# Linear attention as one pipeline over both entries, and the experts' weights and gates made in another order

## The reference, cut to what matters

```
# layer 2, first half (t has 4096 tokens of 128 channels for each of 2 entries)
t = t + linear_attention(layernorm(t))
    q = z @ Wq + bq;  k = z @ Wk + bk;  v = z @ Wv + bv
    kv = sum over the 4096 tokens of k * v          # one number per channel and entry
    result = q * kv
# layer 2, second half: spectral filters; layer 3, first half: causal attention
# layer 3, second half
t = t + experts(layernorm(t))
    p = softmax(z @ router_w + router_b)            # 8 experts
    top 2 of 8, their p divided by their sum        # the gates
    result = sum over the 2 of gate * (z @ expert_w[e] + expert_b[e])
```

## Time and profile before

| | us |
|---|---|
| median of 3 runs | 3167.96 (3166.44 to 3173.08) |
| profiled execution, its own time | 3164.15 |
| profiled execution, span of its instructions | 3162.4 |
| mean granted TensorE clock of it, share of full speed | 0.958 |
| TensorE busy, share of the span | 91% |
| VectorE, ScalarE, GpSimd busy | 61%, 45%, 34% |

### The profile page before, as it was taken

The page is one execution under the profiler, slowest core; times in us unless marked ns, Lnnn a source line. Parts: engine busy times, 40 slices in busy tenths (PEclk is TensorE's granted clock), DMA queues, the critical chain, the costliest instruction groups (busy, mean ns, idle before and its releaser), DMA issues. The chain is left out here.

```text
span 3162.4 us, 61588 instructions
## 1 busy us (share of the span) xinstructions
PE 2886.2 (91%) x23047; PEld 2268.1 (72%) x23047; DVE 1931.8 (61%) x3810; ACT 1436.7 (45%) x3075; POOL 1081.1 (34%) x1115
## 2 busy tenths in 40 slices
PE   5889999499976789999999999999779998999699
PEld 4667777234432559999999999899568887887455
DVE  5555567558844436666666666665457766775465
ACT  2545555221134225555555555554446675666200
POOL 3444444059914035555555555554100000000000
PEclk9999999699988799999999999999879999999699
DMA  7979784000003333444344443442200000000000
GB/s 165 176 171 181 159 182 113 6 9 1 1 3 117 127 75 80 87 84 88 80 86 88 83 89 79 87 88 54 64 7 1 1 1 1 1 1 1 8 24 30
DMA packets 419407, 213.43 MB, mean 67 GB/s; under 512 B 326260, under 2 KB 398604, under 8 KB 417324
## 3 DMA queue, kind: packets, MB, share of 16 engines
q1 hardware_dynamic: 401248, 199.32, 28.8%
q10 hardware_dynamic: 17868, 10.19, 1.7%
HBM read 177.82 MB, written 52.89 MB: 73 GB/s over the span
## 5 line engine op out<-in xcount | busy, mean ns | idle before, releaser
L1754 DVE TENSOR_TENSOR sl_vl_slot<-sl_psV_slot,sl_vh_slot 128x512 fp32r<-128x512 f32 x1024 | 635.7, 683 | 381.3 <-ACT sl_vh_slot L1736 379.4
L1736 ACT ACTIVATE sl_vh_slot<-sl_psV_slot 128x512 fp32r<-128x512 f32 x1024 | 529.6, 604 | 512.0 <-PE sl_psV_slot L1691 511.2
L1709 PE MATMUL sl_psY_slot<-sl_vl_slot,sp_Mh_sp 64*128 64x512 f32 x2048 | 430.8, 389 | 0.8 <-DVE sl_vl_slot L1754 0.3
L1709 PE MATMUL sl_psY_slot<-sl_vh_slot,sp_Mh_sp 64*128 64x512 f32 x2048 | 428.2, 386 | 0.0
L1709 PE MATMUL sl_psY_slot<-sl_vh_slot,sp_Ml_sp 64*128 64x512 f32 x2048 | 428.1, 386 | 0.0
L1667 POOL TENSOR_TENSOR sl_fl_slot<-sl_f_slot,sl_fh_slot 128x512 fp32r<-128x512 f32 x256 | 337.0, 1317 | 20.5
L1665 POOL CAST sl_fh_slot<-sl_f_slot 128x512 fp32r<-128x512 f32 x256 | 167.0, 652 | 450.9 <-PE sl_psV_slot L1691 449.5
L2150 DVE TENSOR_TENSOR ca_ptl_ca<-ca_psT_ca,ca_pth_ca 128x512 fp32r<-128x512 f32 (+1 forms) x272 | 183.8, 676 | 169.1 <-ACT ca_pth_ca L2087 169.1
L2087 ACT ACTIVATE ca_pth_ca<-ca_psT_ca 128x512 fp32r<-128x512 f32 (+1 forms) x272 | 159.0, 585 | 183.4 <-PE ca_psO_ca L87 180.1
L1709 PEld LDWEIGHTS sl_psY_slot<-sl_vl_slot,sp_Mh_sp 64*128 64x128 f32 x2048 | 221.0, 184 | 29.2 <-issue 12.8
L1709 PEld LDWEIGHTS sl_psY_slot<-sl_vh_slot,sp_Mh_sp 64*128 64x128 f32 x2048 | 220.9, 184 | 16.2
(11 more groups left out here) (396 smaller groups left out, 6142.6 us busy)
## 6 DMA issues: line engine op xcount, KB each, us to landing
sl_f_slot<-filt_hat SPq DMA_DIRECT2D x1024, 64.0 KB, 2.2
na_v_na<-na_windows SPq DMA_DIRECT2D x128, 390.0 KB
na_windows<-na_values SPq DMA_DIRECT2D x160, 113.8 KB, 7.3
na_values<-na_vo_na ACTq DMA_DIRECT2D x32, 260.0 KB, 9.0
u_hat<-fw_o_fwd SPq DMA_DIRECT2D x8, 1024.0 KB, 3.8
sl_u_slot<-u_hat SPq DMA_DIRECT2D x128, 64.0 KB, 2.2
y_hat<-sl_y_slot SPq DMA_DIRECT2D x128, 64.0 KB, 1.8
X<-in_x SPq DMA_DIRECT2D x8, 512.0 KB, 7.8
```

What stands on the lines that cost most here:

```text
L1709: mm = e.matmul(psY[half][:, :], left[pl][rows, :], right[pr][rows], start=kc == 0 and k == 0 and x == 0 and z == 0, stop=kc == KC - 1 and ...
L1736: e.activation(v_out(0, n, q), bank(4 * n + q), ACT.Copy).then_inc(S["v_high"], 1)
L1754: e.tensor_tensor(v_out(1, n, q), bank(m), v_out(0, n, q), ALU.subtract).then_inc(S["v_split"], 1)
```

## The change

Linear attention: the loop over entries is gone; there is one stage in which SyncE issues the loads and the other engines wait for them themselves. All 16 chunks of keys and values run in one sequence, and behind each of the chunks of entry 1 comes one query chunk of entry 0; the eight queries of entry 1 come last. There are three buffers `la_t` and three PSUM banks for queries instead of two. The additions to `X` are VectorE's, except that GpSimd has every second chunk of entry 1.

Experts: the loads, the selection tile, the zeroing of the gate images and the bias split run inside the layer norm `ex`, on SyncE and GpSimd (`ExpertInputs`). The gates are made in three spans instead of two: chunks 0 to 2 (12 tiles) ahead of everything, chunks 3 to 7 (20 tiles) within chunks 1 and 2, and entry 1 (32 tiles) four units later than before. The chain of VectorE operations is the same for each span, on as many tiles as the span has.

```diff
+    helper = beside or ahead
-        if beside:
-            beside.begin(sb, S)
+        S = Stage(nc, ctx, names + helper.names if helper else names)
+        if helper:
+            helper.begin(sb, S)
-                    beside.gpsimd(e)
+                    helper.gpsimd(e)
...
 def linear_attention(nc, T):
+    by_pool = lambda c: c >= NCH and c % 2 == 1
+    of_pool = lambda c: sum(by_pool(i) for i in range(c + 1))
+        t_sb = [sb(f"la_t{i}", [128, CH]) for i in range(3)]
+        kvp = sb("la_kvp", [128, B, NCH])
+        kv, bqkv = sb("la_kv", [128, B]), sb("la_bqkv", [128, B])
+        psQ = [pb(f"la_psQ{i}", [128, CH]) for i in range(3)]
+        S = Stage(nc, ctx, ["la_loaded", "k_in_psum_l", "v_in_psum_l", "k_copied", "kv_done", "kv_summed", "bqkv_done",
+                            "q_in_psum_l", "q_scaled", "x_by_dve", "x_by_pool"])
-        with nc.Fori(0, B) as b:
-            cols = lambda c: ds(b * L + c * CH, CH)
-            with S.block() as block:
...
+                def keys_values(c):
+                    if c >= 2:
+                        e.wait_ge(S["k_copied"], c - 1)
+                        e.wait_ge(S["kv_done"], c - 1)
+                    e.matmul(psK[c % 2][:, :], w[:, 1, :], Y[:, cols(c)], start=True, stop=True).then_inc(S["k_in_psum_l"], 1)
+                    e.matmul(psV[c % 2][:, :], w[:, 2, :], Y[:, cols(c)], start=True, stop=True).then_inc(S["v_in_psum_l"], 1)
+                def query(c):
+                    if c >= 3:
+                        e.wait_ge(S["q_scaled"], c - 2)
+                    e.matmul(psQ[c % 3][:, :], w[:, 0, :], Y[:, cols(c)], start=True, stop=True).then_inc(S["q_in_psum_l"], 1)
+                e.wait_ge(S["la_loaded"], 32)
+                for c in range(NC2):
+                    keys_values(c)
+                    if c >= NCH:
+                        query(c - NCH)
+                for c in range(NCH, NC2):
+                    query(c)
...
+                def copy_keys(c):
+                    e.wait_ge(S["k_in_psum_l"], c + 1)
+                    if c >= 2:
+                        e.wait_ge(S["kv_done"], c - 1)
+                    e.activation(k_sb[c % 2][:, :], psK[c % 2][:, :], ACT.Identity, bias=bias[:, 1:2]).then_inc(S["k_copied"], 1)
+                def scale_query(c):
+                    b = c // NCH
+                    if c % NCH == 0:
+                        e.wait_ge(S["bqkv_done"], b + 1)
+                    e.wait_ge(S["q_in_psum_l"], c + 1)
+                    if c >= 3:
+                        if by_pool(c - 3):
+                            e.wait_ge(S["x_by_pool"], of_pool(c - 3))
+                        else:
+                            e.wait_ge(S["x_by_dve"], c - 2 - of_pool(c - 3))
+                    e.activation(t_sb[c % 3][:, :], psQ[c % 3][:, :], ACT.Identity, bias=bqkv[:, b:b + 1],
+                                 scale=kv[:, b:b + 1]).then_inc(S["q_scaled"], 1)
+                e.wait_ge(S["la_loaded"], 32)
+                for c in range(NC2):
+                    copy_keys(c)
+                    if c >= NCH:
+                        scale_query(c - NCH)
+                for c in range(NCH, NC2):
+                    scale_query(c)
...
+                def weigh(c):
+                    b, u = divmod(c, NCH)
+                    e.wait_ge(S["v_in_psum_l"], c + 1)
+                    e.wait_ge(S["k_copied"], c + 1)
+                    if c >= 1:
+                        e.wait_ge(S["kv_done"], c)
+                    e.scalar_tensor_tensor(kv_all[:, :], psV[c % 2][:, :], bias[:, 2:3], k_sb[c % 2][:, :],
+                                           ALU.add, ALU.mult, accum_out=kvp[:, b, u:u + 1]).then_inc(S["kv_done"], 1)
+                    if u == NCH - 1:
+                        e.wait_ge(S["kv_done"], c + 1)
+                        e.tensor_reduce(kv[:, b:b + 1], kvp[:, b, :], AX.X, ALU.add).then_inc(S["kv_summed"], 1)
+                        e.wait_ge(S["kv_summed"], b + 1)
+                        e.tensor_tensor(bqkv[:, b:b + 1], kv[:, b:b + 1], bias[:, 0:1], ALU.mult).then_inc(S["bqkv_done"], 1)
+                def add(c):
+                    e.wait_ge(S["q_scaled"], c + 1)
+                    e.tensor_tensor(X[:, cols(c)], X[:, cols(c)], t_sb[c % 3][:, :], ALU.add).then_inc(S["x_by_dve"], 1)
+                e.wait_ge(S["la_loaded"], 32)
+                for c in range(NC2):
+                    weigh(c)
+                    if c >= NCH:
+                        add(c - NCH)
+                for c in range(NCH, NC2):
+                    if not by_pool(c):
+                        add(c)
+            def _(e):
+                for c in range(NC2):
+                    if by_pool(c):
                         e.wait_ge(S["q_scaled"], c + 1)
-                        e.tensor_tensor(X[:, cols(c)], X[:, cols(c)], t_sb[c % 2][:, :], ALU.add).then_inc(S["q_added"], 1)
+                        e.tensor_tensor(X[:, cols(c)], X[:, cols(c)], t_sb[c % 3][:, :], ALU.add).then_inc(S["x_by_pool"], 1)
...
+class ExpertInputs:
+    names = ["ex_loaded", "eb_high"]
+    def sync(self, e):
+        T, S = self.T, self.S
+        loads = [(self.rw[:, :], T["router_w"]), (self.rb[:, :], T["router_b"][0, :].partition_broadcast(128)),
+                 (self.rank[:, :], T["c_rank"]), (self.ew[:, :, :], T["expert_w"]), (self.eb_in[:, :], T["expert_b"])]
+        for dst, src in loads:
+            e.dma_start(dst, src).then_inc(S["ex_loaded"], 16)
+        e.wait_ge(S["ex_loaded"], 16 * len(loads))
+        e.dma_start(self.eb_in[MOE:2 * MOE, :], T["expert_b"][0:MOE, :]).then_inc(S["ex_loaded"], 16)
+    def gpsimd(self, e):
+        S, ident = self.S, self.T["ident"]
+        e.tensor_tensor(self.pick[:, :], ident[:, 0:MOE], ident[:, MOE:2 * MOE], ALU.add)
+        for b in range(B):
+            e.memset(self.gates[b][:, :, :], 0.0)
+        e.wait_ge(S["ex_loaded"], 96)
+        e.tensor_copy(self.eb[0][:, :], self.eb_in[:, :]).then_inc(S["eb_high"], 1)
+        e.wait_ge(S["eb_high"], 1)
+        e.tensor_tensor(self.eb[1][:, :], self.eb_in[:, :], self.eb[0][:, :], ALU.subtract)
...
+def experts(nc, T, E):
...
+    spans = ((0, 0, 3 * TPC, 1), (0, 3 * TPC, NT - 3 * TPC, 3), (1, 0, NT, 4))
+    span_of = lambda c: 0 if c < 3 else 1 if c < NCH else 2
+    pieces = lambda g: sum(s[3] for s in spans[:g + 1])
-        S0 = Stage(nc, ctx, ["ex_loaded", "eb_high"])
-        with S0.block() as block:
...
+                def logits(g, piece):
+                    b, first, tiles, parts = spans[g]
+                    if g >= 1:
+                        e.wait_ge(S["l_taken"], g)
+                    for i in range(piece * tiles // parts, (piece + 1) * tiles // parts):
+                        at = b * L + (first + i) * 128
+                        mm = e.matmul(psL[:, i * MOE:(i + 1) * MOE], Y[:, at:at + 128], rw[:, :], start=True, stop=True)
                     mm.then_inc(S["l_in_psum_e"], 1)
-                    e.wait_ge(S["g_ready"], b + 1)
+                    e.wait_ge(S["g_ready"], span_of(c) + 1)
-                for q in range(4):
-                    logits(0, q * NT // 4, NT // 4)
+                logits(0, 0)
-                    if x == 2 and 1 <= c < 5:
-                        logits(1, (c - 1) * NT // 4, NT // 4)
+                    if c == 1 and x < 3:
+                        logits(1, x)
+                    if x == 2 and 2 <= c < 6:
+                        logits(2, c - 2)
-                    if c == 5:
-                        exponentials(1)
+                    if c in (2, 6):
+                        exponentials(1 if c == 2 else 2)
+                def take_logits(g):
+                    n = spans[g][2]
+                    e.wait_ge(S["l_in_psum_e"], pieces(g))
...
-                    if n == 5 * MOE:
-                        take_logits(1)
-                    if n == 5 * MOE + 4:
-                        take_first()
-                    if n == 6 * MOE:
-                        take_second()
-                    if n == 6 * MOE + 4:
-                        make_gates(1)
+                    for g, start, step in ((1, MOE + 4, 2), (2, 5 * MOE + 4, 4)):
+                        if n == start:
+                            take_logits(g)
+                        if n == start + step:
+                            take_first(g)
+                        if n == start + 2 * step:
+                            take_second(g)
+                        if n == start + 3 * step:
+                            make_gates(g)
                 finish(NC2 - 1)
-            layer_norm_channels(nc, T, X, into(Y), "ex")
-            experts(nc, T)
+            with ExitStack() as last:
+                inputs = ExpertInputs(nc, T, last)
+                layer_norm_channels(nc, T, X, into(Y), "ex", ahead=inputs)
+                experts(nc, T, inputs)
```

(62 more changed lines are left out.)

135 lines of the change are left out of this document (20 added, 115 removed).

## The result

The changed kernel takes 3132.3 us (median of four, 3130.24 to 3134.44), the kernel before on the same chip 3167.2 (3162.06 to 3173.08): a ratio of 0.990, 95% interval 0.989 to 0.991. The forecast was 3140 with a range of 3131 to 3151. The profiled execution took 3134.44 with a span of 3132.4, so 30.0 us of span went, where the steps had added up to 27.6.

The account below looks back on a forecast made before the run. TensorE, busy 91% of the span, was taken as the bound, with gains where it waits. 12.9 + 9.8 + 8.6 + 3.4 - 4.5 - 2.6 = 27.6 us off 3167.96 gave 3140, range 3131 to 3151.

Parts of the forecast that it names:

- the forecast's own 3135 to 3146: Whole kernel: range of the main case, forecast at 0.76, from half of 9 us less to 5 us more gain.
- Linear attention: 12.9 forecast: Linear attention: 59.1 us from first product to last addition becomes 47.0, start 0.75 earlier; bounds 8.9 and 13.6.
- one barrier of 0.75: Start of linear attention: load waits move from SyncE and a barrier into the engines, so the start is 0.75 us earlier.
- the bound without exclusion: Tail of linear attention: if VectorE's and GpSimd's additions may overlap, the last ends at 46.3 us; gain 13.6.
- Exclusion for the whole of both instructions: Tail of linear attention: VectorE's and GpSimd's additions run serially, 2.0 us a pair, four pairs from 38.9, end at 47.0.
- the pipeline streams: Linear attention's second part: TensorE sets the pace, 2.58 us a chunk; rival of not streaming: 3.4 a chunk, 3147, chance 0.09.
- The opening: Experts: loads, zeroing and bias split move into the norm, leaving 0.8 us instead of 10.6 before the logits; gain 9.8.
- logits: Experts, ahead of the loop: 24 matmuls instead of 64 at half clock, 0.215 us each, 5.2 us; gain 8.6, up to 11.3.
- the chain: Experts, VectorE's 22 operations before the transposes: 96 elements instead of 256, 6.0 us instead of 9.4; gain 3.4.
- the lower bound: GpSimd's zeroing in the norm: 3.5 us each, near VectorE's 3.47; the upper end was 8.4 each.
- Given back: 4.5 + 2.6 forecast: Experts' loop: 40 logit matmuls in chunk 1 cost 4.5 us, VectorE's denser bursts 2.6 (bounds 1.7 and 4.0).
- Entry 1's bursts: Experts' loop: entry 1's gate work comes four units later with the same spacing and keeps its price of 2.1 us.

Follow-up runs that it names:

- after_again: The changed kernel without any change, run again beside the kernel before on another chip; 3110.8 us, 0.990 of the kernel before.
- ex_only: Against the kernel before: only the experts and what they moved into the norm are changed, linear attention is the old one; 3128.0 us, 0.995.
- ahead_only: Against the changed kernel: gates back in the two old spans, the experts' inputs still made in the norm; 3115.2 us, 0.991 of the kernel before.
- la_ahead: Against the changed kernel: linear attention's two loads issued in the layer norm ahead of it; 3110.5 us, 0.990 of the kernel before.
- pool_reads: Against the changed kernel: twelve GpSimd additions with both inputs in SBUF, in the norm behind the zeroing; 3119.0 us, 0.993 of the kernel before.
- zero5: Against the changed kernel: the zeroing of both gate images done five times in the norm; 3115.2 us, 0.991 of the kernel before.
- tail_dve: Against the changed kernel: all additions of linear attention on VectorE, none on GpSimd; 3108.7 us, 0.990 of the kernel before.
- la_only: Against the kernel before: only linear attention is changed, the experts are the old ones; 3125.3 us, 0.994.

## Why the prediction held, and where its steps were off

**The sum.** Forecast 27.6 us less; measured 30.0 between the profiles, 31.2 in after_again, 34.9 between the medians of the result. So 3132.3 lies outside the forecast's own 3135 to 3146 and inside the wider 3131 to 3151 by 1.3 us. That the last 3.7 us did not take it out was luck; they did not come back in after_again. By stage the experts were right as a sum (14.7 forecast, 14.8 measured), and linear attention was too small.

**Linear attention: 12.9 forecast, 15.2 measured.** The mechanism was right, the terms were small: 0.7 at the start, 0.7 in the first half, 0.7 in the tail, and 0.3 in the seam behind it, which the forecast had not counted (1.1 us before, 0.8 after). The start: the wait between the norm and the first product went from 4.92 to 3.50 us, 1.4 less and not one barrier of 0.75 (what else went with it is not told apart). The first half took 15.8 instead of 16.5 us, because the full clock was back 4.0 us behind the first product and not 5.4. This is chance and not the change: in ex_only, with the old loop, the first half took 15.5. The last addition ended at 45.6 and not 47.0; half of that is the first half's. From the end of query 7 the tail took 9.2 us, as the bound without exclusion had it (46.3 - 37.1), and not 9.9: this step was mis-sized. I took a pair as 0.69 + 1.23 plus gaps, 2.0 us in a row. In the rows of the result VectorE's addition starts at 971.13 with GpSimd's running until 971.59, lasts 1.00 instead of 0.69, and GpSimd's own stay 1.27: of an overlap of 0.46 us 0.31 was paid, and the pairs kept TensorE's 1.72. Exclusion for the whole of both instructions, on which the 47.0 rested, would have made a pair at least 0.69 + 1.26 = 1.95. The three stretched operations of the earlier trace rows had stood against GpSimd operations of 3.3 us, and I carried their exclusion over to a pair for which it hardly mattered. The second part was exact, 2.57 against 2.58, so the pipeline streams.

**The opening, logits and the chain: 9.8, 8.6 and 3.4 forecast; 9.6, 8.5 and 3.4 measured.** Taking the logits' own price at half clock was right (0.22 each), and ahead_only shows that it did not hang on the seam before them. The zeroing took 3.5 us each as the lower bound said.

**Given back: 4.5 + 2.6 forecast, 6.6 measured, for partly other reasons.** From the first transposes to the residual of chunk 7 the loop takes 92.9 us before and 99.6 after. The logits' 40 products at 0.11 are 4.4 of it. The bursts: from the residual of chunk 0 to that of chunk 2 are 2999.12 - 2973.80 = 25.3 us; less two chunks of 9.64, and less 44 products at 0.11 that stand in them (the second and third piece, 14 each, and the first of the other entry, 16), that leaves 1.2 and not 2.6. Chunk 1 pays 3.4 and chunk 2 gets 2.2 back: the lead that was lost is regained, which a sum of VectorE's work less one lead leaves out. The other 1.2 us are the cold start of the loop. From the transposes to the residual of chunk 0 it took 18.69 us instead of 16.12, less the 12 products of the first piece, because the full clock was back 7.6 us behind the transposes instead of 5.0. Its first two expert products took 1.91 and 1.69 us; before, by the same view, they were shorter:

```profile
2995.84 1.49 PE L2274 MATMUL ex_psO_ex<-ex_zg_ex,ex_ew_ex 128*128 128x512 f32 x2
...
2997.41 1.02 PE L2274 MATMUL ex_psO_ex<-ex_zg_ex,ex_ew_ex 128*128 128x512 f32 x2
```

This term, too, is chance for the most part: with the same loop it was 0.4 us in after_again and nothing in la_ahead. That two errors of 1.2 and 1.4 us cancelled within the 7.1 forecast and 6.6 measured was luck. Entry 1's bursts kept their price, 2.0 against 2.1.

**The clock rival** was wrong as priced, but something of it is real. Seven profiles have the opening and the loop of the kernel after. In four of them (after_again, ex_only, la_ahead and pool_reads) the granted clock fell to 0.50 for 10.2 us of chunk 1, and came back while the loop went on; in the other three (after, zero5 and tail_dve) it did not. Stretches of 3 us of after_again: length, busy PE, PEld, DVE, ACT, POOL, granted clock, DMA:

```profile
2947.00:2950.00 3.00, 3.00 (x19) 2.17 (x17) 0.79 (x3) 0.00 (x0) 0.00 (x0) 1.00 0.02 5
2950.00:2953.00 3.00, 3.00 (x18) 2.39 (x17) 1.25 (x2) 0.00 (x0) 0.00 (x0) 0.76 0.23 87
2953.00:2956.00 3.00, 3.00 (x14) 2.48 (x13) 0.00 (x0) 0.00 (x0) 0.00 (x0) 0.50 0.00 0
2956.00:2959.00 3.00, 3.00 (x8) 1.76 (x9) 1.57 (x4) 0.00 (x0) 0.00 (x0) 0.50 0.00 0
2959.00:2962.00 3.00, 3.00 (x9) 1.82 (x8) 1.68 (x5) 0.82 (x2) 0.00 (x0) 0.54 0.00 0
2962.00:2965.00 3.00, 3.00 (x10) 1.46 (x8) 2.83 (x8) 0.00 (x0) 0.00 (x0) 1.00 0.00 0
```

and the same place of the kernel after, where it did not fall:

```profile
2973.00:2976.00 3.00, 3.00 (x19) 2.31 (x18) 1.45 (x3) 0.00 (x0) 0.00 (x0) 1.00 0.21 83
2976.00:2979.00 3.00, 3.00 (x19) 2.27 (x18) 1.30 (x4) 0.00 (x0) 0.00 (x0) 1.00 0.01 4
```

TensorE is busy 3.00 of 3.00 us in all of them. The fall begins about the end of the second piece of logits. The third piece, in after_again and in the kernel after:

```profile
2953.58 2.99 PE L2300 MATMUL ex_psL_ex<-ex_rw_ex,Y 128*128 128x8 f32 x14
```

```profile
2976.50 1.62 PE L2300 MATMUL ex_psL_ex<-ex_rw_ex,Y 128*128 128x8 f32 x14
```

From norm to end the four take 192.8 to 192.9 us and the three 189.2 to 189.6, so the price is 3.2 to 3.7 us, and the profile of the result happened to be one without it: with the fall some 10 us would have been given back and not 6.6. The idleness that the rival named was not there. The fall goes with the dense pieces of logits (none of the three kernels with the old spans has it: before, la_only, ahead_only), and the first logits at 0.50 had hinted at that; that they cause it is likely and not shown. What decides whether it falls in a given execution stays open. One thing is in the traces: in the four the full clock had come back 5.0 to 6.0 us behind the first transposes, in the three 6.8 to 7.7. Spreading the pieces further apart was not tried.

## What to carry to other kernels

Read a seam by its rows, then ask of each instruction in it which idle engine of the stage before could have done it: that, with a smaller first batch in front of the loop, brought 21.5 us here for 6.6 given back (some 10 where the clock fell). Its three terms could be priced from rows to 0.2 us; what is given back in a loop that two engines share could not. Where two engines exclude each other, price only the time by which their instructions would overlap, and compare it with the pace that a third engine sets. Price a stretch of small matmuls by its own rows at both clocks: here they ran at either, with TensorE busy throughout.
